# An early context summary, a combination by pairs, and sums in PSUM: one edit of an eight-sublayer transformer kernel

## What is computed

```
x = x + tanh(g_xattn[n]) * attention_n(layernorm(x), ctx_2048, ...)
x = x + tanh(g_ffn[n])   * ffn_n(layernorm(x), ...)          # n = 0..3
```

```
def _L3_xattn_ref(Z, kv, decay, W_in, b_in, W_out, b_out, gamma, beta):
    K = sigmoid(decay)
    x = einsum('btd,ed->bte', kv, W_in) + b_in
    states: s = K * s + x_t over the 64 context tokens of a sequence
    proj = einsum('btd,ed->bte', states, W_out) + b_out
    summary = mean(proj, axis=1, keepdims=True)       # one row of 256 per sequence
    y = Z + summary
    return layernorm(y) * gamma + beta                # Z is layernorm(x)
def weight_quant(w): scale = 1 / clip(mean(abs(w)), EPS); return clip(round(w * scale), -1, 1) / scale
```

## Time and profile before

| | |
|---|---|
| median of 3 runs | 1297.01 us (1296.03 to 1298.27) |
| the profiled execution | 1295.21 us, its span 1293.3 us |
| busy | PE 78%, DVE 64%, ACT 47%, POOL 27% |
| chain that ended last | PE 51%, DVE 12%, ACT 10%, issue 7%, POOL 3%, DMA 3% |

### The profile page before, as it was taken

One profiled execution on the slowest core, in us unless ns is written; L12 is line 12 of the kernel. 1 busy time (PEld: TensorE's weight loads), 2 busy tenths in 40 slices (PEclk: granted clock), 3 DMA queues, 4 the chain that ended last, 5 costly groups with the idle time before them and its releaser, 6 DMA issues.

```text
span 1293.3 us, 21000 instructions
## 1 busy us (share of the span) xinstructions
PE 1003.9 (78%) x6279; PEld 759.5 (59%) x6294; DVE 824.5 (64%) x2010; ACT 603.9 (47%) x1263; POOL 349.3 (27%) x412
## 2 busy tenths in 40 slices
PE   2748869918999757777379999778999999986376
PEld 2436769816777443444246556457888888873254
DVE  7846538854666676767756565567554545476985
ACT  3454247625443475778146666442333333232474
POOL 4085634451000115664231322021111110015300
PEclk9968979968999897989589999889999999995599
DMA  6943457762200021221400000000000002100001
GB/s 206 178 132 99 160 164 220 223 191 89 66 18 1 20 60 48 62 58 58 151 9 17 10 9 25 1 25 25 25 25 24 24 14 84 65 17 0 0 17 49
DMA packets 81986, 86.33 MB, mean 67 GB/s; under 512 B 12076, under 2 KB 75327, under 8 KB 81903
## 3 DMA queue, kind: packets, MB, share of 16 engines
q1 hardware_dynamic: 75374, 68.23, 18.4%
q0 software_dynamic: 6528, 17.04, 4.1%
HBM read 60.39 MB, written 24.85 MB: 66 GB/s over the span
## 4 chain that ended last, share of the span: by engine, by line
PE 51%; DVE 12%; ACT 10%; issue 7%; POOL 3%; DMA 3%; another core or an unknown queue 1%; SPq 0%; ACTq 0%; DVEq 0%; POOLq 0%
PE bank L935 12%; PE bank L956 6%; PE bank L2927 3%; PE bank L1884 2%; PE bank L2965 2%; PE bank L1910 2%; PE bank L2571 2%; PE bank L2958 2%; ACT tern L2378 1%; DMA f_back<-f_outputs 1%; PE bank L2165 1%; PE bank L2912 1%; PE bank L2190 1%; PE bank L3368 1%; PE bank L2176 1%
## 5 line engine op out<-in xcount | busy, mean ns | idle before, releaser
L935 PE MATMUL bank<-xhi,whi 128*128 128x512 f32 x256 | 101.9, 398 | 6.0 <-PE bank L956 3.4
L935 PE MATMUL bank<-xlo,whi 128*128 128x512 f32 x256 | 101.0, 395 | 0.0
L935 PE MATMUL bank<-xhi,wlo 128*128 128x512 f32 x256 | 100.9, 394 | 0.0
L876 DVE TENSOR_TENSOR work<-work,bank 128x512 f32<-128x512 f32 x64 | 44.0, 687 | 77.5 <-PE bank L935 76.6
L854 ACT ACTIVATE ahi<-work 128x512 fp32r<-128x512 f32 x64 | 40.5, 632 | 112.2 <-DVE work L876 112.2
L822 POOL TENSOR_TENSOR wlo<-raw,whi 128x1536 fp32r<-128x1536 f32 x8 | 28.1, 3508 | 223.1 <-ACT whi L836 223.1
L956 PE MATMUL bank<-whi,ahi 128*128 128x256 f32 x256 | 72.8, 284 | 11.3 <-DVE alo L878 11.3
L851 ACT ACTIVATE work<-bank 128x512 f32<-128x512 f32 x64 | 38.2, 597 | 85.5 <-PE bank L935 85.3
L878 DVE TENSOR_TENSOR alo<-work,ahi 128x512 fp32r<-128x512 f32 x64 | 48.3, 754 | 44.7 <-ACT ahi L854 44.7
L956 PE MATMUL bank<-wlo,ahi 128*128 128x256 f32 x256 | 72.3, 282 | 0.0
L956 PE MATMUL bank<-whi,alo 128*128 128x256 f32 x256 | 72.3, 282 | 0.0
(11 more groups left out here) (513 smaller groups left out, 2992.4 us busy)
## 6 DMA issues: line engine op xcount, KB each, us to landing
f_got<-f_sorted SPq DMA_DIRECT2D x39, 129.0 KB
f_sorted<-clear_row SPq DMA_DIRECT2D x1, 4992.0 KB, 23.1
f_back<-f_outputs SPq DMA_DIRECT2D x18, 256.0 KB, 2.9
raw<-in_L_ffn_w SPq DMA_DIRECT2D x24, 176.0 KB
tern_raw<-in_L_ffn_gate_w SPq DMA_DIRECT2D x8, 512.0 KB
tern_raw<-in_L_ffn_up_w SPq DMA_DIRECT2D x8, 512.0 KB
tern_raw<-in_L_ffn_down_w SPq DMA_DIRECT2D x8, 512.0 KB
ctx_in<-in_ctx SPq DMA_DIRECT2D x32, 128.0 KB, 2.9
```

The source lines that it names most:

```text
L876: dve.tensor_tensor(act32[0:m, u % 2, :], silu[0:m, u % 2, :], bank[2 + u % 2][0:m, :], ALU.mult).then_inc(s.hid, 1)
L935: mm = pe.matmul(bank[2 * mat + u % 2][0:m, :], up_w(w, slot, mat, c, q), x[:, c, cols], start=j == 0, stop=j == 3 * DC - 1)
```

## The change

1. f0's combination goes by pairs of tiles: eight POOL adds and eight DVE adds of 128x512 instead of sixteen of 128x256; a ring slot holds two tiles; SP issues the bias of the second attention before the combination's loads and its first four context tiles in the middle of them.
2. In the second attention PE's wait for `before` moves behind the 20 weight transposes.
3. The context summary of the fourth attention is computed in f1: its parts stand inside the loop over the 24 weights, at steps 2/3, 12, 17, 19, 21 and 23. Three of four context blocks have a buffer; the fourth is loaded once PE has pooled the first three. SP's early loads for the third attention (`layer2_early.sync`) stand behind the pooling.
4. In f2 the fourth FFN's weights are loaded at the start, ACT's two size sums stand in the first group (units 6 and 7), the total over partitions is made by a round trip of two DMAs instead of a PE product, and DVE's rounding stands in the last group, a step for each unit; gain and offset at unit 7.
5. In the fourth attention, POOL's mask stands before its wait; the shift is made by block and not once for all; PE makes identity times normalised tile plus spread times summary in PSUM (`bank[4]` to `bank[7]`, two blocks in flight), DVE's sixteen adds L3184 are gone, and the statistics and the scaling read PSUM. The FFN's 32 weight transposes (`tensor_turn`) stand behind tile 3 instead of behind tile 15.

```
+                sp.wait_ge(*before)
+                layer3_lead.sync(sp)
...
                 with sp.Fori(0, looped) as i:
                     group(i + 1)
+                layer3_lead.sync_sizes(sp)
...
+                    if routing and u >= UNITS - 2:
+                        layer3_lead.scalar_size(act, u - (UNITS - 2))
...
+                    if isinstance(n, int) and n == groups - 1:
+                        layer3_lead.vector_steps[u](dve)
...
-                for t in range(TILES):
-                    if t >= OUT_RING:
-                        sp.wait_ge(s.acc, t - OUT_RING + 1)
-                    sp.dma_start(y_back[:, t % OUT_RING, :, :], rows[t]).then_inc(s.back[t % OUT_RING], 16)
+                beside.bias_sync(sp)
+                rows = g.outputs[0:K * TOK, :].rearrange("(k c q p) d -> c k p q d", k=K, q=2, p=P)
+                for c in range(TILES // 2):
+                    if c == OUT_RING:
+                        beside.context_sync(sp)
+                    if c >= OUT_RING:
+                        sp.wait_ge(s.acc, c - OUT_RING + 1)
+                    for k in range(K):
+                        sp.dma_start(y_back[:, c % OUT_RING, k], rows[c, k]).then_inc(s.back[c % OUT_RING], 16)
                 beside.behind_sync(sp)
...
-                for t in range(TILES):
-                    pool.wait_ge(s.back[t % OUT_RING], 16 * (t // OUT_RING + 1))
-                    for k in range(1, K):
-                        if k > 1:
-                            pool.wait_ge(s.pair, t * (K - 1) + k - 1)
-                        pool.tensor_tensor(y_back[:, t % OUT_RING, 0, :], y_back[:, t % OUT_RING, 0, :], y_back[:, t % OUT_RING, k, :],
-                                           ALU.add).then_inc(s.pair, 1)
+                for c in range(TILES // 2):
+                    pool.wait_ge(s.back[c % OUT_RING], 16 * K * (c // OUT_RING + 1))
+                    pool.tensor_tensor(two(c, 0), two(c, 0), two(c, 1), ALU.add).then_inc(s.pair, 1)
...
-                for t in range(TILES + 1):
-                    if t < TILES:
-                        dve.wait_ge(s.pair, (t + 1) * (K - 1))
-                        dve.tensor_tensor(X[:, t, :], X[:, t, :], y_back[:, t % OUT_RING, 0, :], ALU.add).then_inc(s.acc, 1)
-                    if t:
-                        dve.wait_ge(s.acc, t)
-                        next_stat(dve, t - 1)
+                for c in range(TILES // 2 + 1):
+                    if c < TILES // 2:
+                        dve.wait_ge(s.pair, c + 1)
+                        dve.tensor_tensor(flat(X[:, 2 * c:2 * c + 2, :]), flat(X[:, 2 * c:2 * c + 2, :]), two(c, 0), ALU.add).then_inc(s.acc, 1)
+                    if c:
+                        dve.wait_ge(s.acc, c)
+                        for t in (2 * c - 2, 2 * c - 1):
+                            next_stat(dve, t)
                 dve.sem_inc(done, TILES)
...
-                pe.wait_ge(*before)
                 pe.wait_ge(weight.loaded, was.loaded + 16 * 5)
...
                 pe.wait_ge(weight.ready, was.ready + DC * len(weights))
+                pe.wait_ge(*before)
...
+                sp.wait_ge(norm.tp, (norm.first_tp + BLOCKS) * DC)
+                for i in range(BLOCKS):
+                    if i == 3:
+                        sp.wait_ge(m.pooled_ps, 1)
+                    sp.dma_start(context_in[i][:, :, :], block_of(io["ctx_2048"], i)).then_inc(m.here, 16)
+                sp.wait_ge(m.pooled_ps, 2)
                 layer2_early.sync(sp)
...
+            def scalar_summary(act, q):
+                if q == 3:
+                    act.wait_ge(weight.turned, was_w.turned + 1)
+                    act.activation(flat(w_in), bank[4][:, :], ACT.Copy).then_inc(weight.ready, 1)
+                    act.activation(flat(w_out), bank[5][:, :], ACT.Copy).then_inc(weight.ready, 1)
+                if q == 17:
+                    act.wait_ge(m.pooled_ps, 2)
+                    act.activation(pooled_rows, bank[7][0:BATCH, 0:D], ACT.Copy).then_inc(m.pooled, 1)
+                if q == 19:
+                    act.wait_ge(m.pooled_ps, 3)
+                    act.activation(flat(pooled), bank[7][:, D:D + DC * BATCH], ACT.Copy).then_inc(m.pooled, 1)
+                if q == 21:
+                    act.wait_ge(m.state_ps, 1)
+                    act.activation(flat(state), bank[4][:, 0:DC * BATCH], ACT.Copy).then_inc(m.state, 1)
+                if q == 23:
+                    act.wait_ge(m.summary_ps, 1)
+                    act.activation(router_rows["f0"][0:BATCH, :], bank[5][0:BATCH, 0:D], ACT.Copy).then_inc(m.state, 1)
+            def tensor_summary(pe, q):
+                if q == 2:
+                    pe.wait_ge(weight.loaded, was_w.loaded + 16 * 4)
+                    for j, w in enumerate((raw_in, raw_out)):
+                        for c in range(DC):
+                            for a in range(DC):
+                                tp = pe.transpose(bank[4 + j][:, c * D + a * P:c * D + (a + 1) * P], w[:, a, c * P:(c + 1) * P], ident[:, :])
+                    tp.then_inc(weight.turned, 1)
+                if q in (12, 17):
+                    if q == 12:
+                        pe.wait_ge(scan.chain, scan.ready)
+                    pe.wait_ge(m.here, 16 * (3 if q == 12 else 4))
+                    for i in range(3) if q == 12 else (3,):
+                        for k in range(BT):
+                            b = 2 * (i * BT + k)
+                            mm = pe.matmul(bank[7][0:BATCH, 0:D], scan.strip[:, BATCH - 2 - b:2 * BATCH - 2 - b], context_in[i][:, k, :],
+                                           start=b == 0, stop=b == BATCH - 2)
+                    mm.then_inc(m.pooled_ps, 1)
+                if q == 19:
+                    pe.wait_ge(m.pooled, 1)
+                    for c in range(DC):
+                        tp = pe.transpose(bank[7][:, D + c * BATCH:D + (c + 1) * BATCH], pooled_rows[:, c * P:(c + 1) * P], ident[0:BATCH, 0:BATCH])
+                    tp.then_inc(m.pooled_ps, 1)
+                if q == 21:
+                    pe.wait_ge(m.pooled, 2)
+                    pe.wait_ge(weight.ready, was_w.ready + 2)
+                    for r in range(DC):
+                        for c in range(DC):
+                            pe.matmul(bank[4][:, r * BATCH:(r + 1) * BATCH], w_in[:, c, r * P:(r + 1) * P], pooled[:, c, :], start=c == 0, stop=False)
+                        mm = pe.matmul(bank[4][:, r * BATCH:(r + 1) * BATCH], bias_in[0:1, r * P:(r + 1) * P], scan.totals[0:1, :],
+                                       start=False, stop=True)
+                    mm.then_inc(m.state_ps, 1)
+                if q == 23:
+                    pe.wait_ge(m.state, 1)
+                    for c in range(DC):
+                        pe.matmul(bank[5][0:BATCH, 0:D], state[:, c, :], w_out[:, c, :], start=c == 0, stop=False)
+                    pe.matmul(bank[5][0:BATCH, 0:D], ones[0:1, 0:BATCH], bias_out, start=False, stop=True).then_inc(m.summary_ps, 1)
...
                 for q in range(3 * E):
                     scalar_weights(act, q)
+                    scalar_summary(act, q)
...
                 pe.wait_ge(router.kept, router.all_kept)
                 pe.wait_ge(s.tern, ternary.PER * E)
                 for q in range(3 * E):
+                    tensor_summary(pe, q)
...
+            def scalar_size(act, m):
+                if m == 0:
+                    act.wait_ge(whole.raw, was.raw + 32)
+                act.activation(tern[:, m, :], raw_m[:, m, :], ACT.Abs, accum_out=size_sum[:, m:m + 1]).then_inc(whole.size, 1)
+            def sync_sizes(sp):
+                sp.wait_ge(whole.size, was.size + 2)
+                sp.dma_start(sizes, size_sum).then_inc(whole.raw, 16)
+                sp.wait_ge(whole.raw, was.raw + 48)
+                sp.dma_start(all_sums, sizes.rearrange("q m -> (q m)").partition_broadcast(P)).then_inc(whole.total, 16)
...
+            def vector_op(m, op):
+                def step(dve):
+                    link, v = links[0], raw_m[:, m, :]
+                    if op == 0:
+                        link(dve.tensor_scalar(v, v, per_mean[:, m:m + 1], MAGIC, ALU.mult, ALU.add))
+                    elif op == 1:
+                        link(dve.tensor_scalar(tern[:, m, :], v, MAGIC, -1.0, ALU.subtract, ALU.max))
+                    else:
+                        dve.tensor_scalar(tern[:, m, :], tern[:, m, :], 1.0, None, ALU.min).then_inc(whole.tern, 1)
+                return step
+            w.vector_steps = [vector_means] + [vector_op(m, op) for m in range(2) for op in range(3)]
...
+                pool.wait_ge(*before)
                 norm.gpsimd_stats(pool)
...
+                def shifts(i):
+                    tiles = slice(i * BT, (i + 1) * BT)
+                    dve.wait_ge(norm.rstd, norm.all_there - TILES + (i + 1) * BT)
```

(17 more changed lines are left out.)

187 lines of the change are left out of this document (67 added, 120 removed).

## The result

The changed kernel takes 1304.72 us (median of 5 runs, 1301.32 to 1309.37) against 1297.01 for the kernel before on the same chip; the ratio is 1.0071 (95% interval 1.0051 to 1.0091). On a second chip, where the kernel before takes 1277.9 us, the ratio is 1.0075 (1.0055 to 1.0095). The medians alone give 1.0059, inside that interval. The change makes the kernel slower by about 0.7%, 8 to 9 us; the forecast was 1293.8 us, 0.25% faster, with a range that ended at 1303. The profiled execution of after took 1302.08 us with a span of 1300.3, 7.0 over the span before.

A forecast was written before the change was run, and what follows sets the result against it. Nothing was taken as quite full; PE was busy 78% and made half of the last-ending chain. Terms -1.6 -5.2 +12.3 +0.6 +2.8 -12.1 = -3.2 us took the median 1297.0 to 1293.8, range 1286 to 1303.

The forecast's parts named there:

- The fourth attention: From T, the end of f2's last statistics, to ACT's L3307: 57.3 us before, end at T+45.2 after, gain 12.1.
- full for the next four: Fourth attention: products of the four tiles after the first four run at full PE clock, 3.7 us.
- My rival for this part, half the clock throughout: Fourth attention: PE at half clock throughout, gain 7.1 and not 12.1, total +1.8, 1298.8 us; chance 0.20.
- The rule of the Trainium skill: Fourth attention: DVE ops reading PSUM cost 65 ns more than from SBUF, about 1 us less gain; left out of the sum.
- f1's term: f1's loop: the summary's parts make the inverse start at 489.5 instead of 477.1, a loss of 12.3 us.
- The rival of the half clock there: f1's loop from step 12: PE's clock falls to 0.50 in the waits, total +7.5, 1304.5 us; chance 0.13.
- f2's term: f2's last group: DVE's rounding ops make `hid` and `alo` late for PE, a loss of 2.8 us.
- The transposes: Second attention: 20 weight transposes go under f0's combination, PE's first tile at about 292.0 instead of 297.90, gain 5.2 us.
- The pairs: f0's combination by pairs: loads at f1's 317 GB/s gain 2.4 us, less costs at the end, net gain 1.6.
- my lower bound: f0's combination: gain 0 if DVE, busy for 4.31 of 5 us, is what binds.

The follow-up runs named there:

- the first repaired kernel: Changed kernel with rounding between `hid` and `alo`, inverse before step 14, earlier fourth-block load, later state and summary, spread products first in PSUM: 1261.1 us, ratio 0.9872.

## Why the prediction was wrong

**The fourth attention is the step that failed:** "End T+45.2, gain 12.1". It was T+53.1, and the stretch gained 4.2; of the 7.9 us, 3.5 lie ahead of the end of the second block's statistics (T+21.0 and not T+17.5) and 4.4 in the tail behind it (32.1 us and not 27.7). PE's start was right (T+2.98 against T+2.95). Three things were sized wrong.

First the product: 0.89 and 0.475 us came from rows in which products of one kind follow each other; in alternation they take 1.15 and 0.63. Against the 7.4 and 3.7 us that I took, this makes the first two blocks late by 1.8 and 1.3 us; the run with the spread products first shows that it is the order. (My sum has slips of its own: eight products at 0.89 are 7.1 and not 7.4, eight at 0.475 are 3.8 and not 3.7, and the terms for a clock down throughout give T+21.7 and not T+22.1. None of them changes the outcome.)

Second the clock: "full for the next four" held in this trace, but for tiles 8 to 15 I charged 0.8 and assumed PE to be beside DVE. They ran at the half clock, 9.2 us a block against the 3.75 and 1.4 us of DVE's L3302 and L216 that lie beside them, and DVE waited 2.67 and 2.66 us. How much of this is the clock and how much the alternation is known for the last block alone: at the same half clock, with the products grouped, the wait is 0.88.

Third the order: I saw that PE needs the normalised tile for the identity product, but not that the spread product needs none. In the changed kernel it stands behind the identity product, and PE idles for 6.19 us up to T+2.98, in which it could have been made.

My rival for this part, half the clock throughout, gave a gain of 7.1 us. It is what happened in the two profiles in which the second block ran at the half clock too, and there the stretch took 60.8 us against 60.4 before: no gain at all, because the rival's price of a product had the same fault. So even the 4.2 us of the trace of after are partly luck with the clock.

The rule of the Trainium skill ("VectorE: DVE Perf Modes", section on the TRN2 errata) that I weighed there is not borne out by the trace of after either: L3298 reads a bank and takes 1.62 us for four, and L3200 took 1.63 from SBUF.

**f1's term was right:** 12.3 forecast, 11.6 measured, and by the steps that I worked out. The rival of the half clock there was real in part: the same kernel took 2.5 us more in the profile in which PEclk was 0.73 at the loop's end, 14.1 over the kernel before.

**f2's term** was 2.8, and over the eight profiles of kernels with this part unchanged it measured 2.5 to 3.7; its place (PE waiting at the last unit, 2.94 us) was right.

**The transposes** brought 5.8 us at their place in the traces for 5.2 forecast, though the two parts together brought only 3.7 us (1.4 to 5.9) on the kernel before. **The pairs** brought nothing for 1.6: I took f1's combination at 317 GB/s for what the DMAs would do here, and after the change the window 275 to 280 did show 340 GB/s, but the last statistics came no sooner. In the trace of after DVE was busy for all 5.00 us of 285 to 290, and some of its adds took 1.7 us beside POOL's instead of 0.69; that fits my lower bound (0, DVE binds), but no run shows what binds there.

With the measured sizes the sum is -4.7 +11.6 +3.5 -4.2 = +6.2, and +0.8 from the rest makes the 7.0 of the traces. The forecast of this sum was -3.2: of the 10.2 us between, 7.9 are the fourth attention, 2.1 the combination with the transposes (6.8 forecast, 4.7 measured), and the 0.2 left the other parts. The slow rival of f1 at the half clock (0.13) was not what decided, and none of my cases had the fourth attention gain as little as 4 us.

## What to carry to other kernels

Move a chain of small products ahead only to a place where what is queued behind it doesn't wait; look for the engine whose inputs are ready and who waits for the instruction behind the lump (here DVE, 14.4 us), and let that instruction pass first. Before a sum moves from DVE into PSUM, price the product in the order in which it will stand, at both clocks, since the same code ran at either. An operand that is there early should be used first, in runs of one kind.

## What the runs showed of the hardware

- An fp32 product of 256 columns takes 0.48 us at 2.4 GHz and 0.89 to 0.93 at 1.2 GHz among products of its kind, 0.63 and 1.15 where 32-row and 128-row weights alternate.
- The same instructions of the fourth attention ran with their second block at 2.4 GHz in some profiles and at 1.2 GHz in others, 56.2 against 60.8 us. With the sums on DVE the stretch took 44.4 us though the clock was 0.51 throughout.
- Behind a wait of 3.16 us PE ran at 1.2 GHz for 19 us in which it was busy 18.59 us, with bf16 transposes and fp32 products of 32 columns; from two steps behind a wait of 2.37 us for 10 us; in both the clock was back at about the inverse's 32 f16 products, and then stayed up with the same mixture for the steps that were left.
- Two tiles in one bank can have open sums at once if only the first starts (`start=t % 2 == 0`, the first repaired kernel); with both starting, a part of the sum is lost (the run with the spread products first). The Trainium skill ("PSUM — Partial Sum Buffer", section "The four PSUM rules") says that a start clears the flags of the whole bank in the rows that it writes, and these two runs agree with it.
- An op of DVE on 128x4 elements (L3274) took 2.30 us beside GpSimd's add of 128x1024 (L3249), and 0.16 without it.
